# Own grams copied to token-major rows that the selector matmuls read contiguously, with other work of the recurrence at other leaves

## The reference

```
y = S @ k_t
err = y - v_t
S = a_t * S - (b_t * err) outer k_t
o_t = S @ q_t
```

## Time and profile before

| | us |
|---|---|
| median of 3 runs | 3709.59 |
| lowest and highest | 3709.11, 3717.68 |
| the profiled execution | 3708.62 |
| its span | 3706.9 |
| busy in the span: PE, DVE | 3351.2, 2638.9 |
| busy in the span: ACT, POOL | 1461.7, 1213.1 |

### The profile page before, as it was taken

The page is one execution under the profiler, slowest core; times in us unless marked ns, Lnnn a source line. Parts: engine busy times, 40 slices in busy tenths (PEclk is TensorE's granted clock), DMA queues, the critical chain, the costliest instruction groups (busy, mean ns, idle before and its releaser), DMA issues. The chain is left out here.

```text
span 3706.9 us, 50282 instructions
## 1 busy us (share of the span) xinstructions
PE 3351.2 (90%) x15480; PEld 2358.2 (64%) x15480; DVE 2638.9 (71%) x5876; ACT 1461.7 (39%) x3126; POOL 1213.1 (33%) x1388
## 2 busy tenths in 40 slices
PE   5999996699999999999999999999999999978888
PEld 3555553577767777777776767777777777634444
DVE  5777775688787787877878787888888778522222
ACT  3666664244333343434344333344433334311110
POOL 1666665233333232333333333333333333300000
PEclk9999998798989998989999989999999999979999
DMA  2655656322211121211122211122211121020000
GB/s 74 247 226 205 258 206 239 73 52 41 42 35 36 37 57 36 46 36 35 36 53 41 44 38 36 35 53 42 45 37 35 36 45 26 13 83 17 17 17 17
DMA packets 431900, 255.18 MB, mean 69 GB/s; under 512 B 400080, under 2 KB 414128, under 8 KB 416944
## 3 DMA queue, kind: packets, MB, share of 16 engines
q1 hardware_dynamic: 431680, 252.42, 24.5%
HBM read 147.40 MB, written 104.99 MB: 68 GB/s over the span
## 5 line engine op out<-in xcount | busy, mean ns | idle before, releaser
L744 POOL TENSOR_TENSOR B_WT<-B_WT,B_G 128x128 f32<-128x128 f32 (+2 forms) x224 | 145.1, 648 | 1316.1 <-issue 1316.1
L245 DVE SCALAR_TENSOR_TENSOR A_acc<-A_psY,A_w,A_acc 128x410 f32<-128x410 f32 (+1 forms) x720 | 419.3, 637 | 156.0 <-ACT A_acc L285 156.0
L1031 ACT ACTIVATE B_WL<-B_psT 128x128 f32<-128x128 f32 (+2 forms) x480 | 150.3, 313 | 950.7 <-PE B_psT L1405 950.6
L1302 PE MATMUL B_ring<-B_OWN,B_source 128*128 128x64 f32 (+2 forms) x2176 | 523.0, 405 | 0.8 <-DVE B_OWN L868 0.8
L1302 PEld LDWEIGHTS B_ring<-B_OWN,B_source 128*128 128x128 f32 x2176 | 376.3, 217 | 84.5 <-issue 53.0
L949 DVE TENSOR_TENSOR B_NC<-B_NC,B_psM 128x256 f32<-128x256 f32 x480 | 200.5, 418 | 255.5 <-PE B_psM L1426 200.0
L345 PE MATMUL A_psY<-A_xT,A_w 128*128 128x413 f32 (+1 forms) x960 | 347.2, 510 | 9.1 <-PE A_psAG L351 7.7
L202 POOL TENSOR_TENSOR A_outs<-A_outs,A_acc 128x410 f32<-128x410 f32 (+1 forms) x240 | 229.3, 987 | 254.6 <-ACT A_outs L293 254.6
L345 PEld LDWEIGHTS A_psY<-A_xT,A_w 128*128 128x128 f32 x960 | 180.2, 189 | 165.5 <-issue 164.2
L1426 PE MATMUL B_psM<-B_BD,B_WL 128*128 128x128 f32 x1536 | 257.7, 312 | 12.5
L1426 PEld LDWEIGHTS B_psM<-B_BD,B_WL 128*128 128x128 f32 x1536 | 211.1, 210 | 86.2 <-ACT B_WL L1031 85.6
(11 more groups left out here) (196 smaller groups left out, 6550.4 us busy)
## 6 DMA issues: line engine op xcount, KB each, us to landing
scr<-A_outs SPq DMA_DIRECT2D x48, 1024.0 KB, 5.5
B_KQ<-scr SPq DMA_DIRECT2D x96, 512.0 KB, 6.5
scr<-A_outag SPq DMA_DIRECT2D x32, 1024.0 KB, 8.1
A_xc<-nbeta SPq DMA_DIRECT2D x18, 1024.0 KB, 8.6
scr<-A_x SPq DMA_DIRECT2D x16, 1024.0 KB, 7.6
B_A<-scr SPq DMA_DIRECT2D x32, 512.0 KB, 4.5
B_C<-scr SPq DMA_DIRECT2D x32, 512.0 KB, 4.5
B_G<-scr SPq DMA_DIRECT2D x32, 512.0 KB, 4.5
```

Source lines behind the costliest of these rows:

```text
L245: nc.vector.scalar_tensor_tensor(a, y, w[:, s, col:col + 1], a, ALU.mult, ALU.add)\
L1302: last = mm(dst[:, :, :, leaf::2], source[:, R * leaf + r:R * leaf + r + 1].to_broadcast([128, 128]), grams_own[:, R * leaf + t0:R * leaf ...
```

## The change

`OWN` loses its second buffer. Two new ScalarE copies per half chunk, `sort_keys` and `sort_queries`, write the masked grams to `KS` and `QS`, in which each token's row is contiguous (leaf parity, head, pair). The selector matmuls read these. The first `kk` bank takes one run of three rows rather than three runs of one, and `X`, `WX` and `FQ` get the order row, parity, head, pair. `row_pairs` becomes three operations of 128, each behind a ScalarE copy. `gate` is cut into four pieces and `decayed_q` into two, spread over GpSimd's list. `wo` 0 goes from leaf 7 to leaf 9. `decays` of the next chunk goes from leaf 13 to 9, its `leaf_diagonals` from 14 to 11 and the first part of its `leaf_solution` from behind leaf 15 to leaf 14. The second half's `leaf_solution` goes from leaves 4, 5, 6 to 5, 6, 7. `update` jobs start one leaf earlier.

```diff
...
-    wo = {7: [("wo", 0)], 11: [("wo", 1)]}
...
+            9: (wo and [("wo", 0)] or []) + (out and [("var", 0)] or []),
...
+            12: ([] if last else [("kk", 0, 0), ("kk", 0, 1)]) + [("update", 0)],
+            13: ([] if last else [("gram", 0)]) + [("update", 1)],
+            14: [("update", 2), ("update", 3)]}
...
+        KS, QS = sb("KS", [128, 2 * R, H * J // 4]), sb("QS", [128, 2, 2 * R, H, J // 2])
...
-            return ap.rearrange("p h (j r) -> p r h j", r=R)
+            return ap.rearrange("p h (n l r) -> p r l h n", l=2, r=R)
...
-            def decayed_q(o):
-
-                leaves = lambda ap: ap.rearrange("p h (j r) -> p h j r", r=R)
+            def decayed_q(o, n):
+
+                r = slice(2 * n, 2 * n + 2)
                 wait(pool, mq, o + 1, 0)
                 wait(pool, sd, o - 1, 1)
-                tt(FQ.rearrange("p (r h j) -> p h j r", r=R, h=H), leaves(Q[:, o % 2]), leaves(F[:, o % 2]), ALU.mult)\
-                    .then_inc(fq.sem, 1)
-
-            def gate(o):
+                tt(FQ.rearrange("p (r l h n) -> p r l h n", r=R, l=2, h=H)[:, r], by_row(Q[:, o % 2])[:, r],
+                   by_row(F[:, o % 2])[:, r], ALU.mult).then_inc(fq.sem, 1)
...
-                tt(OG[:, :, C * (o % 2):C * (o % 2 + 1)], O[:], G[:], ALU.mult).then_inc(og.sem, 1)
+                h = slice(4 * n, 4 * n + 4)
+                tt(OG[:, h, C * (o % 2):C * (o % 2 + 1)], O[:, h], G[:, h], ALU.mult).then_inc(og.sem, 1)
...
+                gates = lambda *parts: [gate(g - 2, n) for n in parts if g >= 2]
                 scale_right(g, 1)
+                gates(0)
                 scale_left(g, 1)
-                if g >= 2:
-                    gate(g - 2)
+                gates(1)
                 scale_right(g, 3)
+                gates(2)
                 scale_left(g, 3)
+                gates(3)
                 block_decays(2 * g + 1)
-                if g:
-                    decayed_q(g - 1)
                 for j in (5, 7, 9, 11, 13):
+                    if g and j < 9:
+                        decayed_q(g - 1, (j - 5) // 2)
...
+                rows = lambda ps: as_rows(ps[:, 0:3 * HJ2].rearrange("p (k x) -> p k x", k=3))
+                wait(dve, nlc, i, 1)
+                ps = rows(take_bank(dve, g if h else g - 1, "kk", h, 0))
+                tt(xr[:, 3], ps[:, 1], ar[:, 1], ALU.mult).then_inc(nl.sem, 1)
+                tt(xr[:, 4], ps[:, 2], rr, ALU.mult).then_inc(nl.sem, 1)
+                wait(dve, nlc, i, 2)
+                ps = rows(take_bank(dve, g if h else g - 1, "kk", h, 1))
+                tt(xr[:, 5], ps[:, 1], ar[:, 2], ALU.mult).then_inc(nl.sem, 1)
...
+                wait(dve, ks, 2 * (g - 1) + h, 1)
+                wait(dve, qs, 2 * (g - 1) + h, 1)
...
+                    elif j in (5, 6, 7):
+                        if j == 5 and g:
+                            y_terms(g - 1, 4)
+                        leaf_solution(here, j - 4)
...
+                    elif j == 14 and more:
+                        mask_gram(g, 0)
+                        leaf_solution(nxt, 1)
...
+            def sort_keys(i):
+
+                h, g = i % 2, i // 2
+                pairs = OWN[:, 4 * h:4 * h + 4]
+                wait(act, ow, g, 2 * h + 2)
+                wait(act, nl, i - 1, 3)
+                wait(act, nlc, i - 1, 2)
+                copy(KS[:].rearrange("p t (h n) -> p t h n", h=H), pairs[:, :, 0].rearrange("p n h t -> p t h n")).then_inc(ks.sem, 1)
+
+            def sort_queries(i):
+
+                h, g = i % 2, i // 2
+                pairs = OWN[:, 4 * h:4 * h + 4]
+                wait(act, ow, g, 2 * h + 2)
+                wait(act, yv, g - 2, 5)
+                copy(QS[:, g % 2, :, :, 4 * h:4 * h + 4], pairs[:, :, 1].rearrange("p n h t -> p t h n")).then_inc(qs.sem, 1)
...
+                copy(X[:, 0, :], ps[:, 0:HJ2]).then_inc(nlc.sem, 1)
+                ps = take_bank(act, g if h else g - 1, "kk", h, 1)
+                copy(X[:, 1:3, :], ps[:, 0:4 * HJ2].rearrange("p (k x) -> p k x", k=4)[:, 0:3:2]).then_inc(nlc.sem, 1)
...
+                    if j == 4:
+                        pairs_copy(2 * g + 1)
+                    elif j == 13 and more:
+                        pairs_copy(2 * g + 2)
...
+                        sort_keys(2 * g + 1)
                         leaf_diagonals(2 * g + 1)
                     elif j == 3:
-                        pairs_copy(2 * g + 1)
+                        sort_queries(2 * g + 1)
...
+                    elif j == 11 and more:
+                        leaf_diagonals(2 * g + 2)
+                        sort_keys(2 * g + 2)
...
-                        o, pairs, width = g - 1, slice(0, 8), HJ
-                        runs = OUT_ROWS[n]
+                        wait(pe, qs, 2 * (g - 1) + 1, 1)
+                        rows, width, runs = QS[:, (g - 1) % 2].rearrange("p t h n -> p t (h n)"), HJ, OUT_ROWS[n]
                     else:
-                        h = job[1]
-                        o, pairs, width = g if h else g + 1, slice(4 * h, 4 * h + 4), HJ2
-                        wait(pe, ow, o, 2 * h + 2)
-                        runs = (((0, 1, 1), (1, 2, 1), (2, 3, 1)), ((0, 2, 2), (1, 3, 1)))[n]
-                    grams_own = OWN[:, o % 2, pairs, 1 if kind == "qk" else 0].rearrange("p n h t -> p t h n")
+                        wait(pe, ks, 2 * g + (1 if job[1] else 2), 1)
+                        rows, width, runs = KS[:], HJ2, (((0, 1, 3),), ((1, 2, 2), (2, 3, 1)))[n]
                     at = 0
                     for r, t0, m in runs:
-                        dst = ps[:, at * width:(at + m) * width].rearrange("p (t h j) -> p t h j", t=m, h=H)
+                        dst = ps[:, at * width:(at + m) * width].rearrange("p (t l x) -> p t l x", t=m, l=2)
                         for leaf in range(2):
-                            last = mm(dst[:, :, :, leaf::2], source[:, R * leaf + r:R * leaf + r + 1].to_broadcast([128, 128]),
-                                      grams_own[:, R * leaf + t0:R * leaf + t0 + m], start=True, stop=True)
+                            last = mm(dst[:, :, leaf], source[:, R * leaf + r:R * leaf + r + 1].to_broadcast([128, 128]),
+                                      rows[:, R * leaf + t0:R * leaf + t0 + m], start=True, stop=True)
                         at += m
...
```

194 lines of the change are left out of this document (99 added, 95 removed).

## The result

The changed kernel takes 3810.31 us (median of four executions, 3801.25 to 3812.74) against 3709.35 us for the kernel before, measured beside it. The ratio is 1.0262, with a 95% interval from 1.0239 to 1.0285. The forecast was 3684 us, with a range to 3750 us: wrong in sign, and outside the range. The profiled execution has a span of 3805.9 us.

What follows compares the result with a forecast made beforehand. TensorE was taken as the bound only in places, VectorE in most leaves between. Terms of -0.4 us (even chunks) and +1.65 us (odd) gave 20 us over 32 chunks, plus 4.7 us at the end: 3708.6 to 3684 us, range 3580 to 3750.

Steps and rivals of the forecast that it cites:

- TensorE's own numbers: Selectors and `kk` sets: faster contiguous selectors and fewer `kk` instructions take 7.5 us per chunk from TensorE.
- Rival (d): Selectors don't get faster, only fewer `kk` instructions remain, no gain at the end: about 3705 us; chance 0.08.
- (a): Rival: GpSimd and ScalarE are cheap, `decayed_q` at its old rate and sorts at 0.62 us: 3602 us; chance 0.20.
- Leaves 0 to 3: Chunk's first stretch: selector gain, ScalarE sorts and shorter stalls sum to 0, with 1 us either way.
- the cover that I named: VectorE's `decays`, masks and `y_terms` beside the selectors of leaves 0 to 2, making their gain zero in leaves 1 and 2.
- Leaves 4 and 5: 12.73 us becomes 12.2 us, 0.55 us gained, with all 4.2 us of both `decayed_q` halves charged.
- Leaves 6 and 7: TensorE is the bound with work left alone; the third part of `leaf_solution` fits in 3.55 us of idle time: gain 0.
- rival (c): Slower clock: waits in leaves 1 to 5 carry the lower level into `oc` 1, 2 us per chunk: 3748 us; chance 0.22.
- Leaves 8 to 12: Even chunks lose 0.7 us to `decays` at leaf 9 and 1.35 us at leaf 12; `wo` covers both in odd chunks.
- Leaves 13 and 14: 7.25 us becomes 8.7 us, 1.45 us lost, through waiting for TensorE's round and a later `P` copy.
- leaf 15 with the passage: Last leaf and passage to the next chunk: the mask and five steps are gone, 2.55 us gained.
- The end: After the last chunk: the last five `qk` banks run with nothing beside them, 4.7 us gained once.

Runs made afterwards that it cites:

- e1_fill: The changed kernel with unused matmuls added where TensorE waits, four in `oc` 0 (leaf 5) and two at `var` (leaf 9); 3724.77 us.
- e13: e12 with three unused matmuls added at the head of the `gram` 3 job, at each chunk's start; 3618.98 us.
- e14: e13 with query rows kept pair-major, so that `qk` selectors step over 128 floats and ScalarE's copy of them is contiguous; 3658.28 us.
- e5: The changed kernel with the next chunk's `decays` back at leaf 13, `leaf_diagonals` at 14 and `leaf_solution` parts after leaf 15; 3766.29 us.
- e12: e6 with three unused matmuls in `oc` 0 and leaf 9 reordered: `var` first, then `wo` 0 (odd chunks) or `decay` 2 and 3 (even); 3627.57 us.
- e6: The changed kernel with `decayed_q` as one operation with contiguous reads and the decays back at leaf 13, no matmul added; 3661.34 us.
- e11: The changed kernel with `decayed_q` as one operation at its old place, but with the change's stepped reads; 3733.29 us.
- e9: e6 with unused matmuls added, three in `oc` 0 and, in even chunks, two at the head of `var` in leaf 9; 3673.58 us.
- e15: e12 with decays, diagonals and solutions where the change has them (decays at leaf 9); 3620.83 us.
- e2: The changed kernel with `decayed_q` as one operation with contiguous reads, once a chunk at its old place; 3694.76 us.

## Why the prediction was wrong, point by point

**TensorE's own numbers** held: 388 ns for a selector (1.99 us for eight; 2.04 forecast). Its busy time fell by 116 us and not by the 240 us of 7.5 us a chunk, since what runs at half clock counts double. With the clock up more, e1_fill has 2266 us, and some 4 us of filler a chunk are in that: less these, an estimated 2140 us, and the 240 us are there. Rival (d) is out, and so is (a): the sorts took 1.16 us each, as forecast, and the halves more than forecast. **Leaves 0 to 3**, forecast at 0, gained 1.0 us: leaf 2 went from 5.05 to 3.69 us, and leaf 3, which could win by the forecast, from 4.31 to 4.70. For leaf 2, e13 against e14 (3.66 for 4.72 us) shows that the selectors set leaf 2, and not the cover that I named. **Leaves 4 and 5**, forecast -0.55 us, gave -0.28. Each half of `decayed_q` took 2.4 us, 4.7 ns an element, where the nearest row had 4.1 and I took 2.1 us as the upper bound. What I did not ask is when the second half ends, and what TensorE does then.

**Leaves 6 and 7** is the step that failed: "`oc` 1 and leaf 7's merge, which the change leaves alone. ... Gain 0." The work was left alone, its clock was not. It cost 2.57 us a chunk, 80 us. This was rival (c), which I had at 2 us and 3748 us with a chance of 0.22, naming "more waits in leaves 1 to 5" and `oc` 1. The mechanism and the size per chunk were right, the chance was too small. The row for it stood in the earlier trace rows: 1.91 us for two L1339, right behind a wait. A kernel in which the clock already falls each chunk, from which one takes TensorE's work in the leaves ahead and to which one adds stalls, will drop its clock elsewhere; I should have asked where, and it had then been the likeliest case.

**Leaves 8 to 12** is the second failing term: 0.7 us in even chunks for leaves 8 to 11, where the mean of even chunks is 3.4 us (4.5 in chunk 16), and 0 in odd chunks, where it is 0.9. In chunk 16 leaf 9 took 1.9 us more (1.6 in the mean of even chunks), all six decay operations on VectorE's path (0.58 us each in that chunk, beside GpSimd's scaling, 0.39 alone). That part is no clock. Leaf 11 took 3.1 us more there (2.2 in the mean of even chunks), the own grams at half clock, which no case of mine had. The decays' place costs 44 us in all (e5), but little of it through leaf 11, which took 6.0 us with the decays back at leaf 13. In odd chunks `wo` 0 behind `var` ends that fall (e12); in even ones its cause stays open. Leaf 12, forecast 1.35 us in even chunks, took 1.15 us more, with a wait of 0.84 us for `P` in chunk 16 as told.

**Leaves 13 and 14** lost 1.34 us for 1.45, and **leaf 15 with the passage** gained 2.20 for 2.55. **The end** gained 4.3 us for 4.7 (from leaf 15 of the last chunk to the end, 487.4 to 483.1 us). So five of the seven stretches came within 1 us. The sum missed by the other two: by the clock in leaves 6 and 7, and by the clock and the decays in 8 to 12.

How much of the 101 us is the clock can't be given as one number, since the repairs overlap: filler alone returned 86 us, shorter and contiguous GpSimd work alone 116 us, both 133 us. What stays open is why the fall comes in one chunk and not in the next at the same place (leaf 11 of even chunks in e12 is 4.05 us in ten chunks and 5.7 to 6.3 in four), and why it comes in all 14 even chunks of e6 and in 5 of the kernel before, behind the same jobs.

## What to carry to other kernels

Before taking work from TensorE, mark in the windows where its clock stands low and which engine is the bound there. With the fall of the clock in leaves 4 and 5 (the kernel before, e11), leaves 6 and 7 took 9.2 us; with the fall on TensorE's longest job (the changed kernel) they took 11.75. Where TensorE must wait, or has only one-column matmuls, put real jobs that have slack there (`wo` 0 in odd chunks of e12); filler helps while it lies inside the wait and costs its time outside (e9: two matmuls, some 1.3 us, and leaf 10 was 1.2 us longer). And don't judge an edit by its gain in a kernel whose clock is down: the same rows were worth nothing in one kernel and 39 us in the other.

## What the runs showed of the hardware that I had not expected

- The clock can fall with hardly a wait ahead: sixteen one-column matmuls that the profile shows as 1.84 us busy were followed by eight own grams at 3.65 us for 1.99, with no wait over 0.20 us between them (e6, chunk 16). The own grams were slow so in all 14 even chunks of e6, but in 5 of 14 of the kernel before. With 3.7 us of `wo` between, they were slow in none of 13 odd chunks (e12 to e15); with 1.0 us of `decay` transposes, in 4 (e12) and 7 (e15) of 14 even ones.
- A GpSimd product of 1024 elements takes 2.37 us with contiguous reads and 4.45 us when both are read with a step of 32 bytes (e2, e11). The stepped writes of e2 cost nothing: L720 of the kernel before, with no step between neighbouring elements, took 2.36 us.
- TensorE reads 256 columns with a step of 512 bytes between elements in 639 ns (e14), as slowly as with the 1024 bytes of the kernel before (640 ns), and contiguous ones in 388 ns.
- The same stepped work of GpSimd, cut and placed otherwise, made 2.1 us a chunk: in one piece ahead of leaf 5's scaling, leaves 4 to 7 took 22.1 us (e11); in two pieces 24.2 us (changed).
